# Top-2 expert results in a fused two-layer kernel: two plain scatters and a sum, or accumulating scatters onto a cleared array

## What is computed

```python
x = L0_attn_x
xn = _layernorm(x)
x = x + _L0_attn_ref(xn, ...) * _silu(_L0_ffn_ref(xn, ...))
xn = _layernorm(x)
s = _L1_attn_ref(xn, ab, h_0)                       # convolution by FFT, 1024 points
...
router_logits = einsum('bth,eh->bte', xn, router_w)
topk_values, topk_indices = top_k(router_logits, 2)
topk_weights = softmax(topk_values)
h1 = gelu(einsum('bth,efh->btef', xn, w1) + b1, approximate=False)
expert_outputs = einsum('btef,ehf->bteh', h1, w2) + b2
mixed_output = sum(take(expert_outputs, topk_indices) * topk_weights)   # y: two terms for each token
x = x + s * _silu(mixed_output)
```

## Time and profile before

| what | us |
|---|---|
| median of 3 runs | 1532.05 |
| lowest and highest | 1529.40 and 1535.38 |
| the profiled execution, as timed | 1529.39 |
| its span, from the first to the last instruction | 1527.6 |
| experts, first scatter to last | 1210.6 to 1484.2 |
| combine, first load to the end of the span | 1489.0 to 1527.6 |

### The profile page before, as it was taken

One profiled execution on the slowest core, in us unless ns is written; L12 is line 12 of the kernel. 1 busy time (PEld: TensorE's weight loads), 2 busy tenths in 40 slices (PEclk: granted clock), 3 DMA queues, 4 the chain that ended last, 5 costly groups with the idle time before them and its releaser, 6 DMA issues. The chain is left out here.

```text
span 1527.6 us, 29402 instructions
## 1 busy us (share of the span) xinstructions
PE 1291.2 (85%) x8092; PEld 664.9 (44%) x8092; DVE 1011.7 (66%) x2343; ACT 855.0 (56%) x1661; POOL 555.4 (36%) x543
## 2 busy tenths in 40 slices
PE   5889999999999999999988999748885499999970
PEld 2433433433343343333332334224442488888760
DVE  1878888888888888888867886234443144445447
ACT  0277777777777777777766776212221244444432
POOL 2122333342242333334223224455555144444440
PEclk9999999999999999999999997668997699999995
DMA  6322203212212220321220332258773223222219
GB/s 222 96 100 104 100 31 108 106 55 69 106 55 73 103 95 32 110 106 54 69 107 16 110 92 61 77 207 284 250 242 123 63 77 92 78 67 65 61 56 330
DMA packets 116390, 162.27 MB, mean 106 GB/s; under 512 B 17873, under 2 KB 52369, under 8 KB 116050
## 3 DMA queue, kind: packets, MB, share of 16 engines
q1 hardware_dynamic: 103842, 137.73, 28.0%
q0 software_dynamic: 8448, 17.58, 3.3%
q10 hardware_dynamic: 4016, 6.05, 1.3%
HBM read 104.20 MB, written 49.77 MB: 101 GB/s over the span
## 5 line engine op out<-in xcount | busy, mean ns | idle before, releaser
L774 DVE TENSOR_REDUCE row_max<-ps_max 128x2 f32<-128x1024 f32 x512 | 620.6, 1221 | 151.8 <-PE ps_max L1033 149.8
L983 ACT ACTIVATE probs<-ps_exp 128x512 f32<-128x512 f32 x1024 | 559.4, 602 | 228.4 <-PE ps_exp L1033 212.3
L1033 PE MATMUL ps_exp<-q_op,k_op 32*128 32x512 f32 x1024 | 319.2, 503 | 7.4 <-ACT probs L983 6.8
L1033 PEld LDWEIGHTS ps_exp<-q_op,k_op 32*128 32x128 f32 x1024 | 139.3, 184 | 360.1 <-ACT probs L983 310.7
L1115 PE MATMUL ps_y<-probs,v_aug 128*32 128x512 f32 x2048 | 280.9, 618 | 4.5 <-issue 4.5
L1033 PE MATMUL ps_max<-k_op,q_op 32*128 32x512 f32 x1024 | 254.8, 498 | 2.8 <-DMA k_op<-k_parts_scratch 2.0
L1571 ACT ACTIVATE hidden<-ps_h,b 128x256 f32<-128x256 f32 x268 | 118.4, 473 | 161.0 <-PE ps_h L1545 154.5
L1614 POOL DMA_INDIRECT y_scratch<-result,goes_to x134 | 128.4, 958 | 158.1 <-DVE result L1599 137.2
L670 POOL TENSOR_TENSOR rstd<-var_eps,minus_half 128x4 f32<-128x4 f32 x32 | 32.8, 1026 | 321.0 <-DVE var_eps L769 321.0
L315 POOL DMA_INDIRECT sorted_scratch<-rows,place x120 | 116.5, 971 | 88.8 <-issue 32.0
L1552 PE MATMUL ps_o<-w,hidden 128*128 128x128 f32 x1072 | 132.0, 277 | 0.0
(11 more groups left out here) (185 smaller groups left out, 1496.8 us busy)
## 6 DMA issues: line engine op xcount, KB each, us to landing
q_op<-q_parts_scratch SPq DMA_DIRECT2D x16, 1024.0 KB, 5.7
k_op<-k_parts_scratch SPq DMA_DIRECT2D x16, 1024.0 KB, 8.6
q_op<-k_pad_scratch SPq DMA_DIRECT2D x15, 1024.0 KB
k_op<-k_pad_scratch SPq DMA_DIRECT2D x15, 1024.0 KB
unit_rows<-sorted_scratch SPq DMA_DIRECT2D x136, 66.0 KB
q_parts_scratch<-qk_split SPq DMA_DIRECT2D x16, 512.0 KB, 3.1
k_parts_scratch<-qk_split SPq DMA_DIRECT2D x16, 512.0 KB, 2.9
q_parts_scratch<-qk_split SPq DMA_DIRECT2D x16, 256.0 KB, 2.4
```

The costliest lines, as they stand in the source:

```text
L774: dve.tensor_reduce(row_max[group // 2][:, t, head:head + 2], ps_max[u][:, :, :], AX.X, ALU.max)\
L983: act.activation(probs[s % 2][:, i, :], ps_exp[i % 2][:, :], ACT.Exp).then_inc(exp_done, 1)
L1033: return pe.matmul(out, lhsT, rhs, start=True, stop=True)
```

## The change

All rows, of the first and of the second choice, now carry the plain number of the token, and the scatter of L1614 becomes an accumulating one (`compute_op=ALU.add`): it adds the row onto what `y` holds. `y` has 8192 rows and 2048 for the fillers (18432 before, 10240 now). For that:

- SyncE clears `y` in the last body of layer 0 with one DMA of 10240 rows of 512 bytes (5.24 MB) from `zeros`, and waits for it at the end of the block.
- GpSimd, before the first unit of each expert but the first, waits until both scatters of the unit before have landed. A token's two experts are different, so no two scatters in flight touch the same row; inside one expert the waits are as before.
- `combine` loads one array, 16 loads instead of 32, has no `mix`, ScalarE waits for the load itself, and there are three `gate` buffers instead of two.

```diff
--- before.py
+++ after.py
@@ -60,7 +60,7 @@
 ROW = C + 4
 MAX_UNITS = 2 * N_TOK // UNIT + E
 SORTED = E * REGION + MAX_UNITS * UNIT
-Y_ROWS = 2 * N_TOK + E * UNIT
+Y_ROWS = N_TOK + E * UNIT
 
 
 def place_tables():
@@ -71,7 +71,7 @@
 
     token = T * (np.arange(B * TT) // TT)[None, :] + TT * p + (np.arange(B * TT) % TT)[None, :]
     parts = (np.tile(np.arange(E), (128, 1)), np.tile(np.arange(E) * REGION, (128, 1)), token,
-             2 * N_TOK + 128 * fill + p)
+             N_TOK + 128 * fill + p)
     return np.concatenate(parts, 1).astype(np.float32)
 
 
@@ -280,7 +280,7 @@
         rows, gap, taken, rank, picked = (self.rows[0][b % ROW_SETS], self.rows[1][b % ROW_SETS]), self.gap[p], self.taken, self.rank, self.picked
         self.rows_free(dve, b)
         for k in range(2):
-            dve.tensor_scalar(rows[k][:, :, C], self.token_numbers[:, TT * b:TT * b + TT], float(k * N_TOK), None, ALU.add)
+            dve.tensor_copy(rows[k][:, :, C], self.token_numbers[:, TT * b:TT * b + TT])
         dve.wait_ge(self.gap_exp, b + 1)
 
         self.step_done(dve, dve.tensor_scalar(self.gap_sum[:, :, :], gap[:, :, :], 1.0, None, ALU.add), b, 6)
@@ -433,7 +433,8 @@
             ps_max[1][:, 1, 0:(TT + 1) * E].rearrange("p (t e) -> p t e", t=TT + 1)
         inv_loaded, spec_made, spec_copied, div_step, divided = (
             sem(n) for n in ("inv_loaded", "spec_made", "spec_copied", "div_step", "divided"))
-        inverted, zeros_ready, k_ready, k_stored = (sem(n) for n in ("inverted", "zeros_ready", "k_ready", "k_stored"))
+        inverted, zeros_ready, k_ready, k_stored, y_cleared = (
+            sem(n) for n in ("inverted", "zeros_ready", "k_ready", "k_stored", "y_cleared"))
 
 
         def wait(eng, s, v):
@@ -633,6 +634,7 @@
                 if not exists(b + 1):
                     sp.wait_ge(zeros_ready, 1)
                     sp.dma_start(dram["k_pad"][:, T:], zeros).then_inc(k_stored, 16)
+                    sp.dma_start(dram["y"].rearrange("(n p) c -> p n c", p=128), zeros[:, None, :].broadcast_to([128, Y_ROWS // 128, C])).then_inc(y_cleared, 16)
                     for n in range(ROW_SETS - 1, ROUTED):
                         sp.wait_ge(xn_ready[1], n + 1)
                         route.copy_rows(sp, res, n)
@@ -647,6 +649,7 @@
             bodies(one)
             move_y(B - 1, 1)
             spread_inverses(B - 1)
+            sp.wait_ge(y_cleared, 16)
 
 
         @block.gpsimd
@@ -1611,18 +1614,21 @@
                 for i in range(2):
                     pool.wait_ge(result_ready[i], n + 1)
                     apart(pool, pool_passed)
-                    pool.indirect_dma_start(dram["y"], bass.IndirectOffsetOnAxis(goes_to[i][:, 0:1], 0), result[i][:, :], None)\
+                    pool.indirect_dma_start(dram["y"], bass.IndirectOffsetOnAxis(goes_to[i][:, 0:1], 0), result[i][:, :], None, compute_op=ALU.add)\
                         .then_inc(stored[i], 16)
 
-            total = over_units(pool, one)
+            def before(e):
+                if e:
+                    for i in range(2):
+                        pool.wait_ge(stored[i], 16 * ends[pool][e] + 16)
+                        apart(pool, pool_passed)
+
+            total = over_units(pool, one, before)
             for i in range(2):
                 pool.wait_ge(stored[i], 16 * total + 16)
 
 
-def combine(nc, res, dram, s_all, ops):
-
-
-
+def combine(nc, res, dram, s_all):
 
     with ExitStack() as ctx:
         def sb(name, shape, dt=FP32):
@@ -1631,22 +1637,19 @@
         def sem(name):
             return ctx.enter_context(nc.semaphore(name))
 
-        y_second = [ops[b // 8][b // 4 % 2][:, b % 4, :].bitcast(FP32) for b in range(B)]
-        gate = [sb(f"mix_gate{p}", [128, TT * C]) for p in range(2)]
-        y_first = res.xn[:, :, :].rearrange("p (b t) c -> p b (t c)", b=B)
+        gate = [sb(f"mix_gate{p}", [128, TT * C]) for p in range(3)]
+        y = res.xn[:, :, :].rearrange("p (b t) c -> p b (t c)", b=B)
         s_by_batch = s_all[:, :, :].rearrange("p (b t) c -> p b (t c)", b=B)
         x_by_batch = res.x[:, :, :].rearrange("p (b t) c -> p b (t c)", b=B)
         y_loaded = [sem(f"y_loaded{b}") for b in range(B)]
-        mixed_ready, silu_ready, gated_ready, out_ready, out_stored = (
-            sem(n) for n in ("mixed_ready", "silu_ready2", "gated_ready", "out_ready", "out_stored"))
+        silu_ready, gated_ready, out_ready, out_stored = sem("silu_ready"), sem("gated_ready"), sem("out_ready"), sem("out_stored")
         block = ctx.enter_context(nc.Block())
 
         @block.sync
         def _(sp):
-            y_rows = dram["y"].rearrange("(n p t) c -> p n (t c)", p=128, t=TT)
+            y_rows = dram["y"][0:N_TOK, :].rearrange("(n p t) c -> p n (t c)", p=128, t=TT)
             for b in range(B):
-                sp.dma_start(y_first[:, b, :], y_rows[:, b, :]).then_inc(y_loaded[b], 16)
-                sp.dma_start(y_second[b], y_rows[:, B + b, :]).then_inc(y_loaded[b], 16)
+                sp.dma_start(y[:, b, :], y_rows[:, b, :]).then_inc(y_loaded[b], 16)
             out = dram["out"].rearrange("b (t p) c -> p (b t) c", p=128)
             for b in range(B):
                 sp.wait_ge(out_ready, b + 1)
@@ -1656,29 +1659,22 @@
         @block.scalar
         def _(act):
             for b in range(B):
-                act.wait_ge(mixed_ready, b + 1)
-                if b >= 2:
-                    act.wait_ge(gated_ready, b - 1)
-                act.activation(gate[b % 2][:, :], y_first[:, b, :], ACT.Silu).then_inc(silu_ready, 1)
+                act.wait_ge(y_loaded[b], 16)
+                if b >= 3:
+                    act.wait_ge(gated_ready, b - 2)
+                act.activation(gate[b % 3][:, :], y[:, b, :], ACT.Silu).then_inc(silu_ready, 1)
 
         @block.vector
         def _(dve):
-            def mix(b):
-                dve.wait_ge(y_loaded[b], 32)
-                dve.tensor_tensor(y_first[:, b, :], y_first[:, b, :], y_second[b], ALU.add).then_inc(mixed_ready, 1)
-
             def gate_s(b):
                 dve.wait_ge(silu_ready, b + 1)
-                dve.tensor_tensor(s_by_batch[:, b, :], gate[b % 2][:, :], s_by_batch[:, b, :], ALU.mult).then_inc(gated_ready, 1)
+                dve.tensor_tensor(s_by_batch[:, b, :], gate[b % 3][:, :], s_by_batch[:, b, :], ALU.mult).then_inc(gated_ready, 1)
 
             def finish(b):
                 dve.wait_ge(gated_ready, b + 1)
                 dve.tensor_tensor(x_by_batch[:, b, :], s_by_batch[:, b, :], x_by_batch[:, b, :], ALU.add).then_inc(out_ready, 1)
 
-            mix(0)
             for b in range(B):
-                if b + 1 < B:
-                    mix(b + 1)
                 gate_s(b)
                 finish(b)
 
@@ -1730,7 +1726,7 @@
         weights = ExpertWeights(nc, ctx)
         ends = route_and_convolve(nc, res, dram, s_all, route, ops, weights)
         experts(nc, res, dram, ends, weights)
-        combine(nc, res, dram, s_all, ops)
+        combine(nc, res, dram, s_all)
 
 
 def kernel(**inputs):
```

## The result

The changed kernel takes 1572.43 us (median of 4 runs, 1570.75 to 1575.72) against 1530.72 for the kernel before (4 runs, 1529.28 to 1535.38) on the same chip: the ratio is 1.0278, 95% interval [1.0258, 1.0298], so it is slower by about 42 us. The forecast was 1587, with a range of 1526 to 1690.

A forecast was written before the change was run, and what follows sets the result against it. In `experts` a ring of 4.04 us through each landed scatter was taken as the bound. 1532.05 + 60.3 (scatters) + 0.9 (last landing) + 3.5 (waits between experts) - 10.1 (last stage) gave 1587, range 1526 to 1690.

The forecast's parts named there:

- the ring: In `experts`: landing, cast and product, and GpSimd's start close in 4.04 us; accumulating costs 67 x 0.9 = 60.3 us.
- seven borders: Between experts, GpSimd waits for both landed scatters; half 0 goes 0.5 us late, 7 x 0.5 = 3.5 us.
- clear: On SyncE in layer 0: clearing `y` takes 15 to 18 us, hidden by other work; cost 0, at most 5.
- last stage: In `combine`: sixteen sums gone, 9.6 us, and an earlier first product, 0.4 to 0.5; together 10.1 us saved.
- the 0.9 us of one scatter: In `experts`: the DRAM read before an accumulating write delays each landing by 0.9 us, the middle of 0.7 and 1.1.
- the rival of that name: In `experts`: the accumulating scatter's DRAM read hides, d from 0.08 to 0.3 us, chance 0.12; wholly hidden, 0.08.
- 1539, the estimate worked out from it: Whole kernel: with the skill page's 0.2 us for an HBM access as added landing, 1532.05 + 13.6 + 3.5 - 10.1 = 1539.
- its slack: At the borders between experts: half 0 has 4.94 less 1.25, so 3.7 us, before half 1's turn.
- The 9.6: In `combine`: sixteen sums with their starts, 0.60 us each, are gone, saving 9.6 us.
- The 0.4 to 0.5: In `combine`: the first product starts at about 1493.5 instead of 1495.10, of which 0.4 to 0.5 us is additional gain.
- The clock: In `experts`: TensorE, less busy, spends a third of the time at 1.2 GHz, giving 1630 us; chance 0.08.
- The far dearer scatter: In `experts`: accumulation row by row or longer description adds 1.6 to 2.4 us a scatter, up to 1692; chance 0.12.

The follow-up runs named there:

- the last two pauses: Kernel before plus a 0.54 us zeroing on GpSimd that nothing waits for: ahead of every scatter of `experts`, 1549.99 us; ahead of half 0's alone, 1532.76 us.

## Why the prediction was right, and where its sizes were off

Its direction, its range and the ring that multiplies the cost of a scatter were right. What makes the scatter longer was wrong, so that its size came near in part by luck: a ring put 15.4 us too high and borders put 4.9 too low. The time came out 14.6 us under the forecast (1572.4 for 1587). Against the predicted + 54.6 the span moved by + 41.8. By the terms of the sum:

| term | predicted | measured | from |
|---|---|---|---|
| ring, all units | + 60.3 | + 44.9 | experts of the accumulating scatters alone, less before |
| seven borders | + 3.5 | + 8.4 | experts of after, less those |
| last landing | + 0.9 | + 0.8 | last scatter to first load |
| clear | 0 | 0 | clear alone; SyncE's rows |
| last stage | - 10.1 | - 10.7 | `combine` |
| start of `experts` | 0 | - 1.6 | varies between runs: 1208.5 to 1216 |

**The ring.** "Each us that a scatter takes longer to land is paid 67 times" held: plus 0.21 us gave plus 15.5, plus 0.68 gave 44.9, and with the ring opened by a second set the inner rounds were no longer than with plain scatters. The term that was mis-sized is the 0.9 us of one scatter; 0.68 came in issue to cast, and 0.67 for each unit of `experts`. Worse than its size was its place. I took the 0.9 from the DRAM read in front, by loads against stores, and wrote that the row on GpSimd "grows little from 0.96"; a longer issue was only to "come on top". It was the other way round: the row grew by 0.60, and behind its end only 0.03 to 0.08 us were added in the mean.

**The read.** Does it hide, then? Little was added behind the row in the ring, and that far the rival of that name looks right. The page "DMA: Bandwidth & Descriptors" of the Trainium skill, in its section "Latency and other measured facts", lets the write's receipt dominate and gives an HBM access 0.2 us; the nearly unchanged 1.9 us behind the row would agree with that. But 1539, the estimate worked out from it, fell, since it had no term for a longer row. The same page, in "Anatomy of one DMA — SWDGE (gpsimd) path", calls the generation of descriptors small; here it is 0.96 us of 2.8 for a plain and 1.55 of 3.4 for an accumulating scatter, and 0.60 of the 0.68 that the change added lies in it, so the measurement decides.

The traces say more. A plain scatter lands 1.42 us behind its row in some places and about 1.9 in others. What tells them apart isn't the next scatter's distance, which the last two pauses were meant to test: in this round of before the next row begins 0.83 us behind the end of half 0's row, as in the earlier trace rows, and half 0 has still landed 1.43 us behind it.

```profile
1295.93 0.95 POOL L1614 DMA_INDIRECT y_scratch<-result,goes_to  x1 [1.38 <-DVE result L1599]
1297.71 0.96 POOL L1614 DMA_INDIRECT y_scratch<-result,goes_to  x1 [0.82 <-DVE result L1599]
1298.31 0.15 DVE L1597 CAST goes_to<-tails 128x1 uint32 x1 [0.61 <-DMA y_scratch<-result,goes_to]
```

What goes with it is the load of the next unit's rows. VectorE's copy of the tails lets SyncE issue it; in the round of the earlier trace rows that copy is this row, SyncE issues at 1384.45, and half 1's row ends at 1385.34, 1.07 us behind the copy:

```profile
1384.04 0.23 DVE L1588 COPY tails<-unit_rows 128x2 f32 x2
```

In the eight kernels with plain scatters and one set of buffers, a scatter whose row ended 0.35 to 1.4 us behind such a copy landed at a median of 1.89 us (394 waits; 1.76 in the 42 where the next row began 1.3 us or more behind), and the others at 1.42 (174 waits; 1.42 too in the 31 where it began less than 1.2 behind). No run moved the loads alone, so that they are the cause is likely and not shown. Accumulating scatters with one set landed at 1.90 outside that stretch (255 waits) and at 2.14 in it (9). So at the same distance from the loads an accumulating scatter lands about half a microsecond later behind its row as well, and the read doesn't hide. The ring paid little for that, because half 1 of the loop before had already stood at 1.88, in the place where landings are late, and in the changed kernel nearly all rows end outside it. That was luck for the change, and no step of the forecast.

**The borders.** The gap was foreseen well: half 0 goes 4.17 to 4.63 us behind half 1, 4.2 predicted. What failed is its slack: "4.94 less the 1.25 that two scatters need at least". Those 1.25 held a row of 0.96; with 1.56 they are 1.87 (1339.92 to 1341.79), and the round is 4.72, so the slack is 2.85 and half 0 is 1.3 to 1.8 late instead of 0.5. It is the same mistake a second time: a change of GpSimd's row missing from a term that rests on it. With plain rows the waits cost 4.4 to 6.5 us, nearer to my 3.5.

**The last stage.** The 9.6 is confirmed: a round of 1.33 instead of 1.93. The 0.4 to 0.5 is not. The forecast put the first product at 1493.5, 4.5 us behind the first load (6.1 before); it came 3.21 behind it (1541.44 to 1544.65), 1.3 sooner. The first load had landed 2.55 us behind its issue, where this row of ScalarE begins, and the forecast had put that at 3.8:

```profile
1543.99 0.63 ACT L1665 ACTIVATE mix_gate<-xn_all 128x512 f32<-128x512 f32 x1 [1.26 <-DMA xn_all<-y_scratch]
```

From the last x_all row to the end of the span it took 0.6 us longer, 4.0 instead of 3.4. The two misses offset each other in part, so 10.7 came for 10.1. The transfers kept up.

**The signs.** Issue to cast 3.42 (about 3.7 predicted), round 4.72 (5.0), experts 327 (335), `combine` 28.0 (28.5). VectorE's waits are 195.9 us in 132 (145 predicted): the 145 is the longer landing added to the 63 old waits, but half 0 became a ring of its own, with 1.9 us behind a longer row, and its waits were new. By the last sign the forecast falls if the landing is within 0.2 us of the plain one's: counted from the issue, as the 2.81 was, it is 0.6 later; counted from the row's end it would have fallen.

**The rivals that fell.** The clock stayed at 1.00 in `experts` with TensorE busy 32 to 36 of 40 us. The far dearer scatter (1.6 to 2.4 us) didn't come. The clear was hidden, as said; with nearly twice its size SyncE's next move of y still went at 976.62.

## What to carry to other kernels

Before costing a change of an indirect DMA, look whether its row on GpSimd stands in a ring: if a buffer is refilled only after its own scatter has landed, each tenth of a microsecond of description time is paid in every round, and one more buffer can be worth more than the change itself. Here it turned a loss of 42 us into a gain of 18, of which 13 are what the second set gives the kernel before too. When a term's size changes, go through every other term that was computed from the old row, slack above all.

## What the runs showed of the hardware

- GpSimd writes the descriptors of 128 rows of 512 bytes in 0.96 us for a plain scatter and in 1.56 us for an accumulating one; the queue's packets go from 8448 to 23456 for the same 17.58 MB, and the DMA share in `experts` from 0.23 to 0.45. With two sets of buffers no cost of these packets shows in the inner rounds (3.73 us).
- A plain scatter lands 1.42 us behind its row, but 1.89 if the row ends 0.35 to 1.4 us behind the copy that releases the next loads, whether or not the next scatter is near; an accumulating one lands at 1.90, and at 2.14 there (medians). That the loads cause it is not shown by a run of its own.
- A short zeroing on GpSimd ahead of a scatter that doesn't wait for it delays the scatter by 0.21 us, not by its 0.53; with a wait for its end it costs 1.33.
- Eighteen further loads of registers from SBUF cost GpSimd 9.8 us on the path, 0.55 us a load; without them the first scatter was back at 1208.6 and 1212.1 instead of 1220.
